# Two attention layers in one program: the first layer's head outputs kept with channels on partitions, their sums spread through DRAM, and the second layer's norms made by twelve small VectorE operations

## What is computed

```python
# layer 0: 77 text rows, 179 "ip" rows; both softmaxes per head
text_out = softmax(q_h @ k_h.T * scale) @ v_h
sem      = (softmax(q @ k_text.T * scale) @ text) @ ip.T * scale
ip_out   = (softmax(q_h @ ip_k_h.T * scale + 0.5 * sem) * spatial_mask[:, None]) @ ip_v_h
x        = (text_out + ip_out) @ Wout + bout + x
# layer 1: 252 text rows, 4 "ip" rows
text_out = softmax(q_h @ k_t.T * scale) @ v_t
qsem     = l2norm(probs_t @ text)              # per head and row, x / max(norm, 1e-12)
ip_out   = (softmax(q_h @ k_ip.T * scale + 0.5 * qsem @ l2norm(ip).T) * spatial_mask[:, None]) @ v_ip
out      = (text_out + ip_out) @ W_out + b_out + x
```

## Time and profile before

| | |
|---|---|
| median of 3 runs | 1654.78 us (1651.68 to 1661.64) |
| the profiled execution: its time, and its span from first to last instruction | 1654.13 us, 1652.3 us |
| PE busy | 1585.6 us, 96% of the span |
| DVE busy | 1376.9 us, 83% |
| ACT busy | 990.9 us, 60% |
| POOL busy | 841.0 us, 51% |
| DMA engines, mean busy share over the span | 36.5% of 16 engines for queue q1 |
| chain that ended last | PE 87%, DVE 6%, issue 3% |

### The profile page before, as it was taken

The page is one execution under the profiler, slowest core; times in us unless marked ns, Lnnn a source line. Parts: engine busy times, 40 slices in busy tenths (PEclk is TensorE's granted clock), DMA queues, the critical chain, the costliest instruction groups (busy, mean ns, idle before and its releaser), DMA issues.

```text
span 1652.3 us, 42210 instructions
## 1 busy us (share of the span) xinstructions
PE 1585.6 (96%) x14152; PEld 1409.6 (85%) x14152; DVE 1376.9 (83%) x3937; ACT 990.9 (60%) x2044; POOL 841.0 (51%) x789
## 2 busy tenths in 40 slices
PE   6999999999999999998999999999999999999986
PEld 5888888888888888778888989998899989888965
DVE  4687788888888888876879998999999999999985
ACT  3465555656655565654656666666666666666652
POOL 3234432222233222434767776767776777777663
PEclk9999999999999999998999999999999999999998
DMA  8334444444444444543333323332333323332211
GB/s 225 98 106 122 120 124 127 130 121 124 124 128 122 125 128 124 149 120 88 89 102 94 99 69 102 102 104 78 98 95 102 97 78 103 109 96 67 81 30 43
DMA packets 204224, 175.29 MB, mean 106 GB/s; under 512 B 45441, under 2 KB 203531, under 8 KB 204011
## 3 DMA queue, kind: packets, MB, share of 16 engines
q1 hardware_dynamic: 204010, 172.60, 36.5%
HBM read 112.13 MB, written 60.38 MB: 104 GB/s over the span
## 4 chain that ended last, share of the span: by engine, by line
PE 87%; DVE 6%; issue 3%; ACT 1%; DMA 1%; SPq 1%; POOL 1%; DVEq 0%; POOLq 0%; ACTq 0%
PE MISC L103 26%; PE GP L103 20%; PE NAT L265 10%; PE TR L278 8%; PE PV L324 5%; PE PV L309 4%; PE PV L306 3%; PE PV L327 2%; PE MISC L227 2%; DVE ZP L895 1%; PE MISC L368 1%; PE MISC L466 1%; DVE TMP L779 1%; PE MISC L367 1%; PE MISC L388 1%
## 5 line engine op out<-in xcount | busy, mean ns | idle before, releaser
L540 ACT ACTIVATE P<-TA 128x512 f32<-128x512 f32 x320 | 202.3, 632 | 279.0 <-DVE TA L888 277.6
L984 POOL TENSOR_TENSOR ZS<-ZP 128x256 f32<-128x256 f32 x267 | 253.5, 949 | 205.1 <-DVE ZP L895 204.1
L265 PE MATMUL NAT<-KS,QS 65*128 65x256 f32 x1280 | 300.2, 317 | 3.9 <-DMA KS<-qk_parts 2.5
L103 PE MATMUL GP<-PH,GH 128*128 128x256 f32 (+1 forms) x960 | 248.3, 288 | 21.1 <-DVE ZP L895 20.1
L278 PE MATMUL TR<-QS,KS 69*128 69x256 f32 (+1 forms) x1280 | 260.4, 285 | 4.8 <-DVE TA L888 2.7
L783 DVE TENSOR_REDUCE MX<-NAT 128x2 f32<-128x504 f32 x320 | 216.4, 676 | 53.3 <-PE NAT L265 48.9
L901 DVE SCALAR_TENSOR_TENSOR PM<-P,PH 128x512 f32<-128x512 f32 x320 | 254.8, 796 | 0.0
L215 POOL TENSOR_TENSOR PARTS<-QKF,PARTS 112x508 fp32r<-112x508 f32 (+3 forms) x93 | 119.1, 1280 | 265.0 <-ACT PARTS L568 263.1
L265 PEld LDWEIGHTS NAT<-KS,QS 65*128 65x128 f32 x1280 | 201.2, 192 | 57.1 <-issue 42.6
L103 PE MATMUL GP<-PH,GL 128*128 128x256 f32 (+1 forms) x960 | 242.5, 281 | 0.0
L543 ACT ACTIVATE P<-TR 128x512 f32<-128x512 f32 x320 | 192.4, 601 | 72.3 <-PE TR L278 69.2
(11 more groups left out here) (253 smaller groups left out, 3846.4 us busy)
## 6 DMA issues: line engine op xcount, KB each, us to landing
QS<-qk_parts SPq DMA_DIRECT2D x480, 64.0 KB
KS<-qk_parts SPq DMA_DIRECT2D x480, 64.0 KB
qk_parts<-PARTS SPq DMA_DIRECT2D x128, 224.0 KB, 2.8
CT<-in_ctx_t SPq DMA_DIRECT2D x32, 512.0 KB, 3.9
qk_parts<-PARTS SPq DMA_DIRECT2D x64, 192.0 KB, 2.4
XT<-in_x_t SPq DMA_DIRECT2D x48, 112.0 KB, 2.6
XT<-x_t SPq DMA_DIRECT2D x48, 112.0 KB, 2.4
XB<-in_x SPq DMA_DIRECT2D x16, 320.0 KB, 4.1
```

The source lines that it names most:

```text
L103: ins = e.matmul(out, lhs, rhs, start=(n == 0), stop=(n == len(pairs) - 1))
L265: ins = e.matmul(NAT[s % 2][:, i * T:(i + 1) * T], QS[0:KQ, h, i * 128:(i + 1) * 128], KS[0:KQ, h, :], start=True, stop=True)
L540: e.activation(P[:, s % NP, :], TA[:, s % 2, :], ACT.Exp, scale=SCALE).then_inc(q["exp"], 1)
L984: e.tensor_tensor(ZS[s % NZ][:, :], ZP[:, s % 2, 0:S], ZP[:, s % 2, S:2 * S], ALU.add).then_inc(q["zs"], 1)
```

## The change

In layer 0 the head outputs are no longer turned. They stay as PVS has them, channels on partitions and rows along the free dimension:

- **pv_out** (new, SP, at step HG + 2 of each group): four DMAs, one for each head, send 17 rows of 512 columns of PVS to `head_rows` in DRAM. ACT's next copy into PVS waits for them (`pv_out`) where it waited for PE's transposes.
- **sum_in, rec, rs_out** (new, once a batch at steps 46, 48, 50): SP loads the 20 heads' sums as 80 rows of 128, DVE takes reciprocals and multiplies by the mask rows, SP stores them to `head_sums`.
- **rows_in** (new, SP, steps 52, 54, 56): for each third of the channels one DMA loads the head rows (OT) and one loads the reciprocals, each read 16 times, once for each channel of a head (RB).
- **mul, hi, lo** (steps 54 to 60): POOL multiplies 112 by 512 in place and adds the two halves; ACT makes HT's high part, DVE the low part, straight from OT.
- Gone are the transposes L227 (layer 0's) and L237, ACT's copies L501 and L519, DVE's L909, L912 and layer 0's L755, and POOL's L996 and L1001.

In layer 1 POOL's root is gone; DVE makes the reciprocal root with twelve operations of 128 by 40 (a seed by a shift and a subtraction, three Newton rounds of three), two in each of steps 48 to 53 of a batch, and `inv` is one operation in place of two.

```diff
-           sem=6, v=(10, 14, 18), xb_in=53, num=44, hst=49, htl=50, om=(64, 67), y=(65, 68), yt=(72, 73), out=69, out_t=74)
+           sem=6, v=(10, 14, 18), xb_in=53, pv_out=HG + 2, sum_in=46, rec=48, rs_out=50, rows_in=(52, 54, 56), mul=(54, 56, 58), hi=(55, 57, 59), lo=(56, 58, 60), om=(64, 67), y=(65, 68), yt=(72, 73), out=69, out_t=74)
```

ACT, the copy into PVS and HT's high part:

```diff
-                    if g:
-                        e.wait_ge(q["ont"], g)
+                    if 0 < g <= G1:
+                        e.wait_ge(q["pv_out"], PV_OUTS * g)
+                    elif g:
+                        e.wait_ge(q["ont"], g - G1)
                     e.wait_ge(q["pv"], g + 1)
                     e.copy(PVS[:, 0:width], PV[:, 0:width]).then_inc(q["pvs"], 1)
...
+                    e.wait_ge(q["num"], 2 * n + 2)
+                    e.copy(HT[0][0:w, c, :], OT[0:w, n % 2, 0:S]).then_inc(q["ht_hi"], 1)
```

SP, new:

```diff
+            g = due_group(t, AT0["pv_out"], 0, G1)
+            if g is not None:
+                b, hg = divmod(g, NGRP)
+                if b >= 2 and hg == 0:
+                    e.wait_ge(q["ht_lo"], 3 * (b - 1))
+                e.wait_ge(q["pvs"], g + 1)
+                for j in range(HG):
+                    e.dma_start(pv_h[b % 2, HG * hg + j], PVS[SLOT * j:SLOT * j + D + 1, :]).then_inc(q["pv_out"], 16)
+            b = of0(t, AT0["sum_in"])
+            if b is not None:
+                e.wait_ge(q["pv_out"], PV_OUTS * NGRP * (b + 1))
+                if b:
+                    e.wait_ge(q["rec"], 2 * b)
+                e.dma_start(SUMS[:, 0, :], pv_h[b % 2, :, D, :].rearrange("h (k n) -> h k n", k=4)).then_inc(q["sum_in"], 16)
+            b = of0(t, AT0["rs_out"])
+            if b is not None:
+                e.wait_ge(q["rec"], 2 * b + 2)
+                e.dma_start(sums_h[b % 2], SUMS[:, 1, :]).then_inc(q["rs_out"], 16)
+            for c, off in enumerate(AT0["rows_in"]):
+                b = of0(t, off)
+                if b is not None:
+                    n, h0, h1, p0 = 3 * b + c, (0, 7, 14)[c], (7, 14, H)[c], (0, 0, TWICE_O)[c]
+                    rows = D * (h1 - h0)
+                    if n >= 2:
+                        e.wait_ge(q["ht_lo"], n - 1)
+                    if c == 0:
+                        e.wait_ge(q["rs_out"], 16 * (b + 1))
+                    e.dma_start(OT[p0:p0 + rows, n % 2, :], pv_h[b % 2, h0:h1, 0:D, :]).then_inc(q[f"rows_in{n % 2}"], 16)
+                    e.dma_start(RB[p0:p0 + rows, n % 2, :], sums_h[b % 2, 4 * h0:4 * h1, :].rearrange("(h k) n -> h (k n)", k=4).unsqueeze(1)
+                                .broadcast_to([h1 - h0, D, 2 * S])).then_inc(q[f"rows_in{n % 2}"], 16)
```

DVE, layer 0 and layer 1, and POOL:

```diff
+                e.wait_ge(q["sum_in"], 16 * (b + 1))
+                if b:
+                    e.wait_ge(q["rs_out"], 16 * b)
+                e.reciprocal(SUMS[:, 1, :], SUMS[:, 0, :]).then_inc(q["rec"], 1)
+                e.wait_ge(q["rec"], 2 * b + 1)
+                e.tensor_tensor(SUMS[:, 1, :], SUMS[:, 1, :], MASKR[:, :], ALU.mult).then_inc(q["rec"], 1)
...
+            for n, off in enumerate(AT1["rs"][1]):
+                b = of1(t, off)
+                if b is not None:
+                    root_step(e, b, 2 * n + 1)
...
-                e.tensor_tensor(NRM[:, b % 2, :, own], NRM[:, b % 2, :, own], HALF[:, 0:2 * HG].rearrange("p (a h) -> p a h", a=2), ALU.pow).then_inc(q["nrm"], 1)
+            for c, off in enumerate(AT0["mul"]):
+                b = of0(t, off)
+                if b is not None:
+                    n, w = 3 * b + c, CK - c // 2
+                    o = OT[0:w, n % 2, :]
+                    e.wait_ge(q[f"rows_in{n % 2}"], 32 * (n // 2 + 1))
+                    e.tensor_tensor(o, o, RB[0:w, n % 2, :], ALU.mult).then_inc(q["num"], 1)
+                    e.wait_ge(q["num"], 2 * n + 1)
+                    e.tensor_tensor(o[:, 0:S], o[:, 0:S], o[:, S:2 * S], ALU.add).then_inc(q["num"], 1)
```

More of the change, by code:

```diff
@@ L30 @@
 EPS = 1e-12
+ROOT_STEPS, ROOT_SEED = 12, float(0x5f3759df)
 NP = 8
@@ L116, in whole, with build @@
     return w_dr.rearrange("(k p) n -> p k n", p=128)
-def build(nc, ctx, a, parts_h, sel_h, rows_h, vall, x1, x1_t, out):
+def build(nc, ctx, a, parts_h, sel_h, rows_h, vall, pv_h, sums_h, x1, x1_t, out):
     def tiles(stack):
@@ L194, in build @@
                    "tl tpm texp tp tpt tpts g0 g0s snm sn stm st vm v nat mx nh nm tr sum exp pv pvs ont on "
-                   "rec num hs hst ht_hi ht_lo om y yt yts w_cip w_ip once once_s once_q norm rn vall_out "
+                   "rec pv_out sum_in rs_out rows_in0 rows_in1 num hst ht_hi ht_lo om y yt yts w_cip w_ip once once_s once_q norm rn vall_out "
                    "sel_h clear1 w1_q w1_k w1_v w1_o w1_m w1_hi w1_lo ready pads vfix gr vc gh gl ctn vip_in vip kbd scm sc ph pm gp zp zs "
-                   "cmb sq g0z fill0 nrm fu fexp tx ptt pt")
-    FILLS = 6
+                   "cmb g0z fill0 nrm fu fexp tx ptt pt")
+    FILLS, PV_OUTS = 8, HG * 16
     block = ctx.enter_context(nc.Block())
@@ L219, in _ @@
         for t in range(T0, T1):
[L220 to L230, removed]
-                for i in range(2):
-                    k, free = take(("hst", b, i), (q["ht_lo"], 2 * b + i + 1), t, 1.5 + 0.2 * i)
-                    e.wait_ge(*free)
-                    if i == 0:
-                        e.wait_ge(q["hs"], b + 1)
-                    for c, c0 in enumerate(CO):
-                        ins = e.transpose(k[0:CK, c * 128:(c + 1) * 128], HS[:, i, c0:c0 + CK], IDENT[:, :])
-                    ins.then_inc(q["hst"], 1)
+            g = due_group(t, HG + 5, G1)
+            if g is not None:
+                k, free = take(("on", g), (q["on"], g - G1 + 1), t, 0.5)
+                e.wait_ge(*free)
+                e.wait_ge(q["pvs"], g + 1)
+                for i in range(2):
+                    ins = e.transpose(k[:, i * 128:(i + 1) * 128], PVS[:, i * 128:(i + 1) * 128], IDENT[:, :])
+                ins.then_inc(q["ont"], 1)
             b = of0(t, AT0["sem"])
@@ L359, in _ @@
                 if b is not None:
-                    k, free = take(("hst", B + b, i), (q["ht_lo"], 2 * (B + b) + i + 1), t, 1.4)
+                    k, free = take(("hst", B + b, i), (q["ht_lo"], of_ht(B + b, i)), t, 1.4)
                     e.wait_ge(*free)
@@ L979, in _ @@
                 if s == NZ - 1:
-                    e.wait_ge(q["ont"], G1)
+                    e.wait_ge(q["pv_out"], PV_OUTS * G1)
                 if s >= NZ:
@@ L1244, in program @@
     vall = nc.dram_tensor("v_ip", (B * 4, C), F32, kind="Internal").ap()
+    pv = nc.dram_tensor("head_rows", (2, H, D + 1, 2 * S), F32, kind="Internal").ap()
+    sums = nc.dram_tensor("head_sums", (2, 4 * H, 128), F32, kind="Internal").ap()
     with ExitStack() as ctx:
-        build(nc, ctx, a, parts, sel, rows, vall, x1, x1_t, out)
+        build(nc, ctx, a, parts, sel, rows, vall, pv, sums, x1, x1_t, out)
 def kernel(**inputs):
```

160 lines of the change are left out of this document (83 added, 77 removed).

## The result

The changed kernel takes 1980.6 us (median of four runs, 1980.0 to 1985.0) against 1655.6 for the kernel before: a ratio of 1.197 [1.194, 1.200], slower. Forecast were 1963 us, in a range of 1840 to 2140. The profiled execution is the one of 1980.0 us, with a span of 1978.0.

A forecast was written before the change was run, and what follows sets the result against it. One DMA engine, loaded by 17-row stores, was to replace PE as layer 0's bound at 62.0 us a batch against 43.2: 1654.1 + 301 + 8 for layer 1 = 1963 us, range 1840 to 2140.

The forecast's parts named there:

- The width step: Layer 0's pv_out: 17 rows on both sides have no divisor up to 16 but 1, so each DMA runs on one engine.
- PE's saving: Layer 0: PE loses transposes worth 4.0 us a batch, 64 us in all, which only adds to its idle time.
- The sum of the engine's work: Busiest DMA engine, layer 0: existing 18.5, max_rows 1.6, pv_out 31.7, OT and RB 8.9; sum 60.7 us a batch.
- once a batch the queue runs empty: Layer 0: DVE's reciprocal waits for sum_in, and rows_in for rs_out, each behind four pv_outs; 1.3 us a batch added.
- Where it blocks: Layer 0: ACT may not overwrite the one PVS until pv_out lands, which holds its exponentials and so DVE and PE.
- the 15 us of ACT's waiting: Layer 0 sign: ACT's copy into PVS, its exponentials or HT's high parts wait for a DMA some 15 us a batch.
- PE's share: Sign in the changed profile: PE under 70% busy in layer 0.
- Layer 1: DVE's root steps take 0.5 us a batch beyond its slack, +8 us in all; bounds 0 and 30, no gain possible.
- DVE's 1.9 us a batch: Layer 1: twelve operations add 2.5 us a batch, 0.40 and 0.23 go: +1.9 within 4.3 us of slack.
- The six steps' local overrun: Layer 1: DVE's added work falls in six of 20 steps with 1.3 us of slack; 0.5 us a batch taken.
- wide after all: Rival: pv_out runs wide, a group's stores land in under about 6 us, SP's issues bind; 1627 us, chance 0.07.

The follow-up runs named there:

- rows18: The changed kernel with 18 rows of PVS in each pv_out DMA in place of 17, the 18th unused: 1774.8 us, ratio 1.071 to the kernel before.
- rows19: The changed kernel with 19 rows in each pv_out DMA in place of 17, two of them unused: 2018.2 us, ratio 1.219 to the kernel before.
- one128: The changed kernel with one pv_out DMA of all 128 partitions for a group in place of four of 17 rows: 1760.3 us, ratio 1.061.
- act_queue: The changed kernel with the same 17-row pv_out DMAs issued by ACT on its own queue, behind its copy into PVS: 1897.1 us, ratio 1.145.
- root_only: The kernel before with only layer 1's part of the change, DVE's twelve root steps for POOL's root: 1651.3 us against 1655.3, ratio 0.998.
- wide_in: The changed kernel with one 128-partition store a group, OT and RB loaded with 16 channels outermost, and later reciprocal, third load, products and casts: 1683.1 us, 1.015.

## Why the prediction was right

**The width step: right, and now shown.** 17 rows run on one engine: the window of share 0.06, and the two neighbours 18 and 19. The rule of the Trainium skill (DMA: Bandwidth & Descriptors, "Why a DMA increments its semaphore by 16 and not by 1") gives 1, 9 and 1 engines for 17, 18 and 19 rows; the windows of the changed kernel (0.06) and of rows18 (0.61) agree, and so does the time of rows19. For DMAs that GpSimd issues the Trainium skill (same page, "Anatomy of one DMA — SWDGE (gpsimd) path") fits 2.0 us plus bytes at 436 GB/s. SP issued those of this kernel; carried over to them as an estimate, the fit gives 2.1 us for a store of 17 rows and 2.6 for one128's 256 KB. The wide one took 3.0 us, and behind the narrow ones DVE stood 7.2 us, so it can't be carried over to a store on one engine.

**PE's saving: as forecast, nothing of it is seen.** PE has 64 us less to do in layer 0, and layer 0 grew all the same; no run prices the saving by itself.

**The sum of the engine's work: too large, in one term.** The trace shows 25 GB/s for the lone engine, not 22. With 25 GB/s for both kinds (the loads' own rate was not measured) the stores are then 696/25 = 27.8 us a batch instead of 31.7, the loads 197/25 = 7.9 instead of 8.9, and the sum is 18.5 + 1.6 + 27.8 + 7.9 = 55.8 us instead of 60.7.

**The waits: too small.** The step "once a batch the queue runs empty", 1.3 us, is the one that was mis-sized: 64.2 less 55.8 leaves 8.4 us a batch. The prediction took a saturated engine as a pace and gave its queue no further price. But DVE stands 7.2 us for the sums, and in that time no new maxima, no new P and so no new stores are made. The engine then stands empty itself: the four stores end at 514.3 us, the next are issued at 518.7, and at 519 to 520 us the mean share of the 16 engines is 0.05, at 8 GB/s (the row is in the last section). act_queue takes 83/16 = 5.2 us a batch of this away, by order or by SP's time, and lands at 58.7, near the engine's 55.8. The two errors, −4.9 and +7.1, largely cancel, and that is luck: layer 0 was +301 in the forecast and is +324, while the terms were off by more than their sum.

**Where it blocks: half right.** The prediction hung the loop on the one PVS. ACT waits for it only 3.5 us a batch; the larger waits are those for small transfers behind the stores, the maxima (SP 12.3 us), the sums (DVE 7.2), RB (POOL 12.4, and ACT behind it 13.8). "The row maxima go through the same engine behind pv_out" names one of these, without a price. Of the signs, the 15 us of ACT's waiting came as 17.3, but 13.8 of them before HT's high parts, for POOL, and not at the copy into PVS, on which the prediction's argument hung.

**PE's share: sign missed.** Forecast was under 70% in layer 0; it is 160.4 of 200 us, 80%. By work it would be 38.5 of 64.2 us, 60%, had PE run as before. But the granted clock there is 0.81 instead of 1.00, and an instruction of PE holds it 139 ns (160.38/1154) instead of 108 (42.48/395). SP's issues are 382 us in the 600 from 300 on, 41 us a batch (36 to 39 forecast), under the batch as said.

**Layer 1: wrong in sign, by 12 us.** "A gain is excluded" and "some 0.5 us a batch" both failed. The term that was mis-sized is DVE's 1.9 us a batch. The root steps' durations were sized well (mostly 170 to 200 ns each, 2.2 us a batch for 2.5), but the prediction laid them end to end, and DVE starts its next operation some 0.1 us before such a one ends. ZP, and PM behind it, before; then in root_only with a root step between them:

```profile
1192.59 0.69 DVE L895 TENSOR_TENSOR ZP<-GP,PM 128x512 f32<-128x512 f32 x1
1193.20 0.68 DVE L901 SCALAR_TENSOR_TENSOR PM<-P,PH 128x512 f32<-128x512 f32 x1
```

```profile
1161.42 0.68 DVE L920 TENSOR_TENSOR ZP<-GP,PM 128x512 f32<-128x512 f32 x1
1162.02 0.18 DVE L229 TENSOR_TENSOR NRM<-NRM 128x40 f32<-128x40 f32 x1
1162.12 0.68 DVE L930 SCALAR_TENSOR_TENSOR PM<-P,PH 128x512 f32<-128x512 f32 x1
```

From ZP's start to PM's it is 0.61 us without the step and 0.70 with it: a step of 0.18 us costs 0.1. Twelve cost 1.2 us a batch, and two operations go for one. Another operation became shorter by 1.1 us, the product FU<-ON,NRM, before and in root_only:

```profile
L826 DVE TENSOR_TENSOR FU<-ON,NRM x16: 321/1448/2039, 871.3 to 1637.7; 128x160 f32<-128x160 f32 x16
```

```profile
L851 DVE TENSOR_TENSOR FU<-ON,NRM x16: 315/320/873, 869.4 to 1631.6; 128x160 f32<-128x160 f32 x16
```

But PM became longer, from 791 to 830 ns in the mean of 900 to 1600 us, 0.8 us for the 20 of a batch, so little of that is left. The six steps' local overrun, 0.5 us in the forecast, isn't seen in PE, which waited 6.3 us for ZP in 700 us instead of 8.1. In the changed kernel layer 1's batches are 53.65 us as well (before 53.9), but its first takes 65.6 instead of 60.2 us, and so the part comes out at +0.8 and not at −4; that layer 0's last loads still run into that first batch is a guess that no run tests.

**The rival "wide after all".** Its condition, a group's stores landing in under 6 us, is met in one128 (3.0), but its time of 1627 came from none of the kernels. It would have wanted three things that it didn't name: wide loads, later steps, and whatever holds the rest. (Its 8 us on each of 16 engines is 2.0 MB at the spill's 250 GB/s; at the 22 GB/s that the prediction uses for one engine it is 5.7. Nothing hangs on it.) wide_in is 32 us above root_only, all of it in layer 0 (723.3 against 691.0 us from the first TA to the last), although PE has 64 us less to do there. Half of the 32, 17 us, is lost in the last 40 of layer 0's 320 steps, and 9 in one batch; the batches between take 43.6 us in the middle where root_only's take 43.1. The shares of the chain that ended last, of the kernel before and of wide_in:

```profile
PE 87%; DVE 6%; issue 3%; ACT 1%; DMA 1%; SPq 1%; POOL 1%; DVEq 0%; POOLq 0%; ACTq 0%
```

```profile
PE 66%; DVE 12%; SPq 9%; issue 6%; DMA 3%; POOL 2%; ACT 2%; DVEq 0%; ACTq 0%; POOLq 0%
```

No engine holds it: the chain goes round PE, DVE's maxima, SP's gathers and back. SP is issuing for 34 of 44 us there and in one stretch for 28 us almost without a gap, which speaks for its order; that the store moved to ACT changed nothing speaks against it, but that is only 2 of the 34 us. What sets wide_in's batch of 43.6 us, where PE's work is 39.2, is left open, and so is what a slower PE clock adds in layer 0, since no run held the clock.

## What to carry to other kernels

Before a transfer is priced by its bytes, look at the outermost counts of both sides and their common divisors: 17 rows cost 206 us more than 18. A mean DMA share can't show one full engine; it fell here while DMA became the bound, and what shows it is a stretch with only one kind of transfer in flight. A full engine costs twice, by its own work and by the small transfers that wait behind, and those waits reach every engine that works in order, until the full one runs empty too; so sum both. A right total can hide two wrong terms. A short operation on DVE costs less than its duration, so look at the starts of its neighbours. The repairs don't add, and a chain spaced out too early costs instead of saving.
